# A two-layer attention, feed-forward and expert kernel: the shared expert's order, its last column and the slot steps; the feed-forward's output sum

## What is computed

```
x = x + cross_attention(layernorm(x), ctx)                 # 8 heads' scores summed, one softmax
x = x + bitlinear_ffn(layernorm(x))                        # ternary weights, 8-bit tokens, exact gelu
x = x + latent_attention(ctx, layernorm(x), mask)          # 4 heads of 64
x = x + moe(layernorm(x))

def bitlinear(x, W, b):      # w: sign values times mean|W|; x: rounded to 127 steps of max|x| of the token
    return xq @ wq.T + b

def moe(x):                  # 2048 tokens, 8 experts, the best 2 of each token, and a shared expert
    h(x, w1, b1, w3, b3) = swiglu((x @ w1 + b1) * (x @ w3 + b3))
    swiglu: g = min(even columns, 7); l = clip(odd columns, -7, 7); g * sigmoid(1.702 g) * (l + 1)
    return sum over chosen e of weight_e * (h_e(x) @ w2_e + b2_e)  +  (h_s(x) @ sw2 + sb2)
```

## Time and profile before

| | us |
|---|---|
| median of 3 runs | 968.35 (965.2 to 969.68) |
| the profiled execution | 969.65 |
| its span, first to last instruction | 967.9 |
| TensorE busy | 887.8 (92%) |
| VectorE busy | 644.2 (67%) |
| ScalarE busy | 532.4 (55%) |
| GpSimd busy | 388.1 (40%) |
| mean granted TensorE clock | 0.971 |

### The profile page before, as it was taken

One profiled execution on the slowest core, in us unless ns is written; L12 is line 12 of the kernel. 1 busy time (PEld: TensorE's weight loads), 2 busy tenths in 40 slices (PEclk: granted clock), 3 DMA queues, 4 the chain that ended last, 5 costly groups with the idle time before them and its releaser, 6 DMA issues.

```text
span 967.9 us, 15115 instructions
## 1 busy us (share of the span) xinstructions
PE 887.8 (92%) x4301; PEld 619.7 (64%) x4302; DVE 644.2 (67%) x1296; ACT 532.4 (55%) x848; POOL 388.1 (40%) x321
## 2 busy tenths in 40 slices
PE   8987669889999999999998998989999999999992
PEld 4644436545455555555466787878888888888881
DVE  4698997864466466466388678855666666566656
ACT  2446766536656756665555533424666656566660
POOL 2134433635567647647504544622222222222210
PEclk8997999999999999999999999999999999999997
DMA  9400000006496586577564200059531188516315
GB/s 304 97 1 1 0 0 1 1 1 243 165 378 233 217 341 262 205 314 306 214 240 160 123 1 1 6 185 422 221 133 33 42 330 342 208 53 272 97 37 174
DMA packets 49908, 154.05 MB, mean 159 GB/s; under 512 B 6266, under 2 KB 24438, under 8 KB 44236
## 3 DMA queue, kind: packets, MB, share of 16 engines
q1 hardware_dynamic: 46124, 144.25, 39.5%
q0 software_dynamic: 3744, 9.31, 3.0%
HBM read 97.85 MB, written 56.62 MB: 160 GB/s over the span
## 4 chain that ended last, share of the span: by engine, by line
PE 63%; DVE 19%; issue 5%; DMA 5%; ACT 3%; POOL 2%; SPq 1%; DVEq 0%; ACTq 0%; POOLq 0%
PE banks L1028 11%; PE banks L1279 6%; PE banks L1281 6%; PE banks L1280 6%; PE banks L997 3%; PE banks L1020 3%; DMA aux<-moe_x,small 3%; PE banks L1021 3%; PE banks L935 2%; DVE small L1933 2%; DVE wexp L1946 2%; PE banks L1316 2%; PE banks L1318 1%; PE banks L1317 1%; PE banks L1292 1%
## 5 line engine op out<-in xcount | busy, mean ns | idle before, releaser
L1028 PE MATMUL banks<-wexp 128*65 128x512 f32 (+1 forms) x288 | 149.4, 599 | 2.6 <-ACT wexp L1586 2.6
L662 POOL TENSOR_TENSOR cv_hl<-wexp,cv_hl 128x1024 fp32r<-128x1024 f32 x45 | 108.5, 2417 | 54.0 <-ACT cv_hl L1563 53.4
L1279 PE MATMUL banks<-ring,x_hi 128*128 x312 | 128.2, 411 | 0.0
L1281 PE MATMUL banks<-ring,x_lo 128*128 x312 | 122.6, 393 | 0.0
L1280 PE MATMUL banks<-ring,x_hi 128*128 x312 | 122.4, 392 | 0.0
L1586 ACT ACTIVATE wexp<-banks 128x512 f32<-128x512 f32 x128 | 76.3, 598 | 74.5 <-PE banks L1021 74.2
L2059 DVE TENSOR_REDUCE small<-banks 128x1 bf16<-128x1101 f32 x64 | 83.7, 1307 | 37.8 <-PE banks L997 37.8
L1721 ACT ACTIVATE banks<-wexp 128x1024 f32 x72 | 73.4, 1020 | 47.7 <-DVE aux L2413 47.7
L1699 ACT ACTIVATE aux<-banks 128x512 f32<-128x512 f32 x78 | 46.6, 597 | 64.2 <-PE banks L1281 48.0
L1020 PE MATMUL banks<-q_hi,k_hl 128*128 128x512 f32 x144 | 75.0, 521 | 1.7 <-ACT q_lo L1554 1.0
L730 POOL DMA_INDIRECT moe_y<-aux,small x20 | 20.6, 1030 | 116.3 <-DVE aux L2423 116.3
(11 more groups left out here) (363 smaller groups left out, 2199.5 us busy)
## 6 DMA issues: line engine op xcount, KB each, us to landing
wsplit<-cv_hl SPq DMA_DIRECT2D x45, 1024.0 KB, 8.0
ring<-wsplit SPq DMA_DIRECT2D x32, 1280.0 KB
wexp<-in_L_ffn_w SPq DMA_DIRECT2D x40, 512.0 KB, 5.9
wexp<-in_expert_biases SPq DMA_DIRECT2D x8, 1152.0 KB, 6.4
ring<-wsplit SPq DMA_DIRECT2D x4, 1024.0 KB, 8.5
wexp<-moe_y SPq DMA_DIRECT2D x7, 512.0 KB, 6.4
wexp<-in_L_ffn_sw SPq DMA_DIRECT2D x5, 512.0 KB, 9.8
x_sb<-in_x SPq DMA_DIRECT2D x4, 512.0 KB, 8.0
```

Source lines behind the costliest of these rows:

```text
L662: g.tensor_tensor(sides(hl[:, PIECE:2 * PIECE]), raw, sides(hl[:, 0:PIECE]).bitcast(f32), ALU.subtract).then_inc(s['cv_lo'], 1)
L1028: mm(pb[5 + half][0:DA, :], vh[b][0:w, c, :], pT[q % 3][0:w, :], start=c == 0, stop=c == len(KTILES) - 1).then_inc(s['a_pv'], 1)
L1279: mm(o[:], x_hi[u][:, kc, :], hi, start=kc == 0 and not primed, stop=False, skip_group_check=primed)
L1281: last = mm(o[:], x_lo[u][:, kc, :], hi, start=False, stop=primed and kc == KC - 1, skip_group_check=primed)
```

## The change

Feed-forward: the hidden sum is one instruction over both banks; the output's sum of tile i-1 comes first in a turn, its statistics after the step factors.

```diff
-                for half in range(2):
-                    c = slice(half * 512, (half + 1) * 512)
-                    last = v.scalar_tensor_tensor(h_f[u][:, c], pb[2 * (1 - u) + half][:], f_step[:, u, 0:1], b1_all[:, c], ALU.mult, ALU.add)
-                last.then_inc(s['f_acc'], 1)
+                v.scalar_tensor_tensor(h_f[u], banks[:, 2 * (1 - u) * 512:2 * (2 - u) * 512], f_step[:, u, 0:1], b1_all[:], ALU.mult, ALU.add).then_inc(s['f_acc'], 1)
...
             def ffn_turn(i, u):
+                if there(i - 1):
+                    ffn_sum(i - 1, 1 - u)
                 if there(i + 1):
                     ve.wait_ge(s['f_acc'], i + 2)
...
+                if there(i - 1):
+                    ffn_statistics(i - 1)
                 if there(i + 4):
                     last = ffn_tokens(i + 4, u)
-                if there(i - 1):
-                    ffn_finish(i - 1, 1 - u)
```

```diff
-                    pe.wait_ge(s['h_line' if side else 'h_gate'], ci)
+                    pe.wait_ge(s['h_read'], 2 * ci - 1 + side)
...
-                link(v.scalar_tensor_tensor(line, pb[UP_BANK[1][0]][:], bsh[:, 0, ci % IC, 1:2], lift[1], ALU.add, ALU.mult))
-                link(v.tensor_scalar(line, line, LIMIT, -LIMIT, ALU.min, ALU.max))
-                ve.sem_inc(s['h_line'], 1)
+                v.scalar_tensor_tensor(line, pb[UP_BANK[1][0]][:], bsh[:, 0, ci % IC, 1:2], lift[1], ALU.add, ALU.mult).then_inc(s['h_read'], 1)
+                ve.wait_ge(s['h_read'], 2 * ci + 2)
+                v.tensor_scalar(line, line, LIMIT, -LIMIT, ALU.min, ALU.max).then_inc(s['h_line'], 1)
```

```diff
                 if ci > 0:
                     plus_one(ci - 1)
+                    if ci == 2:
+                        tokens_hi(4)
+                        tokens_hi(5)
                     hidden_hi(ci - 1)
-                if ci == 2:
-                    tokens_hi(4)
-                    tokens_hi(5)
+                if ci in (1, 3):
+                    logits_kept(ci)
                 if ci == 4:
+                    lifted_sh(ci, 1)
                     act.wait_ge(s['r_e'], 1)
                     a(score[:], score[:], ACT.Exp).then_inc(s['r_exp'], 1)
                     ready(ACT.Sigmoid)
                 chance(ci)
-                if ci in (1, 3):
-                    logits_kept(ci)
-                lifted_sh(ci, 1)
+                if ci != 4:
+                    lifted_sh(ci, 1)
...
-            plus_one(4 * IC - 1)
             hidden_hi(4 * IC - 1)
...
-            hidden(4 * IC - 1)
+            gated(4 * IC - 1)
...
+            def product_sh(ci):
+                ve.wait_ge(s['h_line'], ci + 1)
+                ve.wait_ge(s['h_sg'], ci + 1)
+                ve.wait_ge(s['h_hi'], ci)
+                ve.wait_ge(s['h_loP'], ci)
+                v.scalar_tensor_tensor(h_sh, line, 1.0, sig, ALU.add, ALU.mult).then_inc(s['h_fP'], 1)
+
+            def low_sh(ci):
+                hi, lo = hb[ci % 8]
+                ve.wait_ge(s['h_hi'], ci + 1)
+                v.tensor_tensor(lo, h_sh, hi.bitcast(f32), ALU.subtract).then_inc(s['h_loP'], 1)
...
-            gate_sh(2)
             tokens_low(4)
             tokens_low(5)
+            gate_sh(2)
             line_sh(2)
...
             gate_sh(4)
+            line_sh(4)
...
-            line_sh(4)
             link(v.tensor_tensor(bg1, theirs, mine, ALU.is_gt))
```

The slot steps are cut into `ring_rows` (the first five), `slots` (the next eleven), `last_tiles` (seven) and `slots_out` (the marker), and spread:

```diff
             weights_of(1)
+            row_places()
+            slot_experts()
             gate_sh(10)
-            row_places()
+            ring_rows()
             tiles_of_places(0)
             line_sh(10)
...
             gate_sh(14)
             result_sh(1, (0, 1))
+            slots()
             line_sh(14)
             result_sh(1, (2, 3))
             indices()
             gate_sh(15)
-            slot_experts()
             line_sh(15)
-            slots()
+            product_sh(4 * IC - 1)
+            last_tiles()
+            low_sh(4 * IC - 1)
+            slots_out()
             result_sh(2)
```

More of the change, by code:

```diff
@@ L707, in _, with gated @@
                    allow_small_or_imprecise_dtypes=True).then_inc(s['r_table'], 1)
+            def gated(ci):
+                pool.wait_ge(s['h_sig'], ci + 1)
+                g.tensor_tensor(sig, sig, gate, ALU.mult).then_inc(s['h_sg'], 1)
             def hidden(ci):
                 hi, lo = hb[ci % 8]
-                pool.wait_ge(s['h_sig'], ci + 1)
-                g.tensor_tensor(sig, sig, gate, ALU.mult).then_inc(s['h_sg'], 1)
+                gated(ci)
                 pool.wait_ge(s['h_sg'], ci + 1)
@@ L1147, in up @@
                         last = mm(o[:], hi, xl[:, kc, tok], start=False, stop=kc == KC - 1)
-                    last.then_inc(s['h_w3' if j else 'h_w1'], 1)
+                    last.then_inc(s['h_up'], 1)
             def index():
@@ L1641, in lifted_sh @@
             def lifted_sh(ci, side):
-                act.wait_ge(s['h_w3'], 2 * ci + side + 1)
+                act.wait_ge(s['h_up'], 4 * ci + 2 * side + 1)
                 if ci > 0:
-                    act.wait_ge(s['h_line' if side else 'h_gate'], ci)
+                    act.wait_ge(s['h_read'], 2 * ci - 1 + side)
                 a(lift[side], pb[UP_BANK[side][1]][:], ACT.Identity, bias=bsh[:, 1, ci % IC, side:side + 1]).then_inc(s['h_lift'], 1)
@@ L1953, in ffn_finish, with ffn_statistics @@
                     .then_inc(s['f_yout'], 1)
+            def ffn_statistics(t):
                 ve.wait_ge(s['f_yout'], t + 1)
@@ L2156, in gate_sh @@
             def gate_sh(ci):
-                ve.wait_ge(s['h_w1'], 2 * ci + 1)
+                ve.wait_ge(s['h_up'], 4 * ci + 2)
                 ve.wait_ge(s['h_lift'], 2 * ci + 1)
@@ L2160, in gate_sh @@
                     ve.wait_ge(s['h_sg'], ci)
-                link(v.scalar_tensor_tensor(gate, pb[UP_BANK[0][0]][:], bsh[:, 0, ci % IC, 0:1], lift[0], ALU.add, ALU.mult))
+                v.scalar_tensor_tensor(gate, pb[UP_BANK[0][0]][:], bsh[:, 0, ci % IC, 0:1], lift[0], ALU.add, ALU.mult).then_inc(s['h_read'], 1)
+                ve.wait_ge(s['h_read'], 2 * ci + 1)
                 v.tensor_scalar(gate, gate, LIMIT, None, ALU.min).then_inc(s['h_gate'], 1)
             def line_sh(ci):
-                ve.wait_ge(s['h_w1'], 2 * ci + 2)
+                ve.wait_ge(s['h_up'], 4 * ci + 4)
                 ve.wait_ge(s['h_lift'], 2 * ci + 2)
@@ L2326, in slots @@
                 link(v.tensor_tensor(r, n, r, ALU.subtract))
+            def slots():
+                n, r, w = (x[0:1, :] for x in (slot_n, slot_r, slot_w))
                 link(v.tensor_scalar(w, r, float(NB), float(BRING - NB), ALU.mult, ALU.add))
@@ L2336, in slots, with last_tiles @@
                 v.tensor_copy(slot_i[:, READY:READY + SLOTS], n)
-                v.tensor_copy(slot_i[:, ENDS:ENDS + E], tend_n[0:1, :])
+                link(v.tensor_copy(slot_i[:, ENDS:ENDS + E], tend_n[0:1, :]))
+            def last_tiles():
                 odd, even = last_n[0:1, 0:1], last_n[0:1, 1:2]
```

7 lines of the change are left out of this document (4 added, 3 removed).

## The result

| | before | after |
|---|---|---|
| median, us | 967.15 (965.2 to 969.68, 4 runs) | 953.51 (951.19 to 955.5, 4 runs) |
| after over before | | 0.9883, interval 0.9848 to 0.9917 |
| profiled execution, its span | 969.65, 967.9 | 951.19, 949.4 |
| VectorE busy | 644.2 | 638.1 |
| mean granted TensorE clock | 0.971 | 0.985 |

The change makes the kernel faster, by 0.8 to 1.5%. It gave a gain of 10.0 us; the medians differ by 13.6 here and by 10.6 in the later set of runs that had both kernels. The measured median happens to lie nearer to the 952.85 of the rival *VectorE keeps up*; the last part says why that rival is not what happened.

A forecast was written before the change was run, and what follows sets the result against it. VectorE was taken to bound the feed-forward, and TensorE's waits the shared expert. Gains of 2.5 and 7.5 us, sum 10.0, took the profiled 969.65 to 959.65, less 1.3 for the median: 958.35 us, range 951.5 to 963.0.

The forecast's parts named there:

- VectorE keeps up: Rival, chance 0.15: lines 13 to 15 stay ahead, shared expert gives 12 of 15.6 us, feed-forward 3.5: 952.85 us.
- The feed-forward, 2.5 us: Feed-forward turns: 4.76 to 4.50 us, 11 x 0.26 = 2.9, less 0.4 in the first turn; bounds 2.0 and 4.5.
- Column 4, 4.0 us less 0.5: Shared expert: line 4 moved ahead wins TensorE's 2.3 us wait and 1.7 of clock; line 5 costs 0.5.
- Columns 1 and 2, about 1.2: Shared expert: 0.70 wait goes, 2.01 shrinks to about 0.8, a new 0.5 before the fourth logits; lead about 1.2 us.
- The release at the read, 0.5 and more per wait: Shared expert: TensorE waits for the instruction reading the bank, not the clip; six waits each at least 0.5 us shorter.
- Lead at column 15: 6.4: Shared expert: lead of about 6.4 us when column 15 starts, with waits of 1.0 and 0.6 at columns 12 and 13.
- Column 14, lead down to 4.5: Shared expert: 11 slot steps, 3.0 us, ahead of line 14, read 1.9 us after TensorE wants the bank; lead 4.5.
- One of my signs of being wrong: Shared expert, column 15: a TensorE wait over 2 us with a low clock behind it would show the forecast wrong.
- The last column, 1.4 + 1.6: End of shared expert: final wait falls from 2.7 to about 1.3 us, and its clock loss of 1.7 goes too.
- The lead is handed on: Routed experts: their weight loads wait for the shared expert's end, so its lead, 7.5 us, should be kept in full.
- VectorE held by GpSimd: Rival, chance 0.15: shared-expert VectorE steps run into GpSimd four times more, 1.0 us each; gain 6.0, time 962.35 us.
- The rival in which the low clock makes turns of 5.6 us: Rival *Slower*, chance 0.04: feed-forward's first sum blocks VectorE's queue at low clock, 9.2 us more; time 973.6 us.

The follow-up runs named there:

- the shared part alone: All of the diff but its feed-forward part, on the kernel before: ratio 0.9927, interval 0.9904 to 0.9950, median 956.94 us.

## Why the prediction was right, point by point

The total was right, mostly for the right reasons and in part by luck: 10.0 us forecast, and 2.3 + 7.85 = 10.2 in the stretches that the change touches, at equal clock. The luck is that errors cancel. In the order of time the shared expert's forecast was 6.4 of lead at column 15, less 1.9, plus 3.0; the runs give 7.5, less 2.6 (what the slot steps gave back when they were put late), plus 2.9 (what the last column cost when undone). The differences of the medians, 13.6 and 10.6, are larger; I put the excess down to the scatter of single executions (the medians of the kernel before alone go from 964.36 to 967.15), which is argued and not shown. The terms:

- **The feed-forward, 2.5 us.** The one sum (1.29, measured 1.28), the turn (4.50, measured 4.50) and the reason that TensorE's path would bind before VectorE's 4.33 all held. The multiplication did not: of the eleven turns nine follow the pattern, the first of them gains 0.19 and the last two (4.77 and 4.15) nothing, so 2.3 for 2.9. The -0.4 for the first turn can't be seen: that turn takes 4.2 us where its granted clock was 1.00 and 6.4 to 6.8 where it was 0.69 to 0.77, and the same code has both 4.24 and 5.54.
- **Column 4, 4.0 us less 0.5.** This is the term that failed as the price of its edit, too large by some 3 us. The lead behind it looks right: the first down product starts 31.8 us behind tokens 4, and 35.7 before, which is 3.9, and with the 0.8 ahead of tokens 4 it is 4.7 for a forecast of 4.6. But undone alone, the order of column 4 costs 0.7 there, that of columns 1 to 3 costs 1.1, and the release at the read 1.4. I took a wait and the low clock behind it as two losses and both as won. Gate 5 was nearly as late as line 4, and the clock cost 0.3 at most. What column 4's order would give without the other edits was not run.
- **Columns 1 and 2, about 1.2.** Under-sized: 1.5 to 1.9 by the undoing. The wait before the fourth logits was 0.22, not 0.5, and the third transposition waited 0.39, not 0.8.
- **The release at the read, 0.5 and more per wait.** Right in kind: with the release undone six of TensorE's waits are 0.4 to 0.8 longer, 3.3 us of lead at column 15. The forecast added it up by itself only from column 9 on; 1.4 of the 3.3 arise before the first down product, and of the whole only 1.7 reach the end.
- **Lead at column 15: 6.4.** Measured at the index product, which stands just ahead (before, then after; tokens 4 start at 518.25 and 507.87):

```profile
616.60 1.35 PE L1155 MATMUL banks<-wexp 128*128 128x78 bf16 x32
```

```profile
599.44 1.35 PE L1159 MATMUL banks<-wexp 128*128 128x78 bf16 x32
```

  That is 98.35 - 91.6 = 6.7, and 0.8 from the stretch ahead of tokens 4 at equal clock (18.99 and 18.20), together 7.5. The waits of 1.0 and 0.6 forecast for columns 12 and 13 did not come; there is one of 0.89 at column 11 and one of 0.29 at column 14.
- **Column 14, lead down to 4.5.** The wait was 2.22 for 1.9: the eleven steps took from 601.06 to 605.01, 3.95 us for 3.0. The third down product started 105.06 us behind tokens 4 before. After, it is 100.9 in the execution with the clock at 1.00, a lead of 4.2 and 0.8, about 5.0; in the one with the low clock it is 102.1 and the lead about 3.7. One of my signs of being wrong, a wait over 2 us at column 15 with a low clock behind it, came true there. The total held since that low clock cost 0.2 us.
- **The last column, 1.4 + 1.6.** Right: undone it costs 2.9, half in the wait and half in the clock. The chain from line 15's clip took 2.6 us (from 613.4 to 616.0) for the 2.9, with the two new instructions at 0.69 each for 0.75.
- **The lead is handed on.** Right as far as the scatter lets one see: from the first routed product to the end it is 324.4 to 328.2 us in all profiles, before (327.6 and 324.4) and after (326.7 and 327.9) alike. The timed runs of the shared part alone give 4.8 to 9.3 us (0.9904 to 0.9950), which fits a lead of 7.85 and excludes one that is lost.

Of the rivals, *VectorE keeps up* wanted lines 13 to 15 ahead of TensorE and 12 us from the shared expert; TensorE waited 2.2 us for line 14 and the stretch gave 7.85, so it did not happen. *VectorE held by GpSimd* was real in kind. At column 14 two slot steps took 1.18 and 1.22 us, each beside a GpSimd instruction:

```profile
600.89 1.30 POOL L723 TENSOR_TENSOR hb<-aux,hb 128x512 fp32r<-128x512 f32 x1 [0.74 <-ACT hb L1664]
602.16 1.29 POOL L712 TENSOR_TENSOR aux<-aux 128x512 f32<-128x512 f32 x1
```

The same two steps took 0.17 each when they stood alone behind the last column. That is the rule that "SBUF — State Buffer", Who interferes with whom, in the Trainium skill gives (an exclusive lock, held for the whole instruction), and the trace agrees: each ended within 0.05 us of the GpSimd instruction. It cost 2 us there, of which the forecast's 3.0 held 0.8 (3.0 less 2.2). The rival's further 4 us did not come: the meetings moved, but there were not more of them. From the first shared to the first routed product 19 instructions of VectorE before and 18 after ran 0.4 us or more over the shortest of the same code and shape in any profile, in all 17.6 us over it before and 15.6 after. The rival in which the low clock makes turns of 5.6 us had no turn of that kind behind the first.

**What stays open.** The undone parts (column 4's 0.6, the release's 1.7 and the last column's 2.9 in the routed column, and 1.5 to 1.9 for columns 1 to 3) add up to 6.7 to 7.1 of 7.85 us. The rest may belong to the row places and slot experts ahead of gate 10, or to the parts together; the ring rows and slot experts were not moved back alone. Nor did any run tell why the clock of the start differs between executions.

## What to carry to other kernels

When two engines take turns at being late, price an edit by the end event of the stretch and not by the waits it removes: here a 2.3 us wait with its low clock was worth 0.7 once the other edits were there, since the engine behind it was almost as late. A low clock cost 0.2 to 0.3 us where another engine set the end afterwards, and 1.5 where TensorE did. Small steps that nobody needs yet belong behind the last thing the critical engine waits for, and where single executions scatter by 5 us, cut the traces at fixed events and compare the pieces.

## What the runs showed of the hardware

- The granted clock of TensorE near the start and in the first feed-forward turns differed between executions of the same code: 10 to 20 us was granted 0.66 and 0.93 in the two profiles of the kernel before and 1.00 twice in the kernel after, and the stretch to the first hidden sum varied by 4.6 us over the 14 profiles. I had taken one profile's low clock as a property of the kernel.
- After TensorE had waited 2.2 to 2.3 us the clock fell in some executions and not in others (column 15: 0.86 and 1.00 over the same 10 us, low in five of eight profiles; line 4: 0.83 and 1.00); after 2.5 to 2.7 us ahead of the last down product it fell in all four profiles, after 0.3 to 1.15 there in none of five.
- One sum of 1024 over two PSUM banks takes 1.28 us, against 0.75 for 512 and 0.47 for 256: it is what the further columns cost (1.29 by that slope), and no price for crossing the bank shows.
